# Attention block: maxima through GpSimd's DMA queue, scores seven pairs ahead, two buffers for the bias tables, slots written out

## The chip, the cores and the metric

The kernel runs on one core of one Trainium2 chip. Its time is device microseconds of one launch. Five engines work in parallel, each through its own instructions in order: TensorE (PE; PEld is its weight load), VectorE (DVE), ScalarE (ACT), GpSimd (POOL) and SyncE (SP), which here does nothing but issue DMAs. They meet at semaphores. Before the change three runs took 1225.28, 1225.32 and 1228.18 us; the median is 1225.32 us.

## The reference

Eight sequences of 512 tokens with 256 features go through a pre-norm layer: attention with 16 heads of 16 features and a bias by relative position, then a mixture of experts. All is float32. The part that matters here:

```
scores = einsum('bhqd,bhkd->bhqk', q, k) * SCALING + position_bias
attn   = softmax(scores, axis=-1)
ctx    = einsum('bhqk,bhkd->bhqd', attn, v)
x = x + ctx @ Wo.T
x = x + ffn(layernorm(x))      # 7 routed experts, two chosen, and a shared one
```

`position_bias` depends on key position minus query position alone, and is constant beyond a distance of about 90.

## The kernel before, in words

There are three stages, each a block that begins when all engines have ended the one before: `project` (norm, q, k, v and the bias tables; they go to DRAM), `attend` (attention) and `finish` (output projection and experts). The change lies in `attend` and in the loads that it shares with `project`.

`attend` handles 32 items, one for each of 8 sequences and 4 groups of 4 heads; item n is done in slot n. Eight items share a head group, so the bias tables of the group change when slots 8, 16 and 24 begin; four items are a quad. A slot has 8 steps; a step is one pair of heads and one block of 128 rows.

The softmax needs the row maxima before the exponentials, and for that the scores are computed twice. `scores` (L766) puts q times k of one head and 128 queries into one of three PSUM banks of `pS`; VectorE (L688) adds the bias from the table `near` and takes the negated maximum of each row into `nmax`. After the 16 units of an item `turn` (L692) splits the maxima into a high and a low part and transposes them, and two DMAs carry them by way of DRAM: `store_max` (L590) and, once that has landed, `load_max` (L597), which puts them as two more rows into `q_st`. `exponents` (L783, L791) computes the scores a second time, transposed, with the maxima and the far bias as additional rows and the near bias added through the table `bandT`; ScalarE takes the exponential (L733) into `prob`, and `values` (L805) multiplies with v one slot later, into `pC`. ScalarE copies `pC` out (`copy_ctx`, L742) and SyncE stores it. GpSimd copies v into its padded form (L670).

TensorE's order is written by hand: in step s of slot n it does the scores that lie LEAD = 5 steps beyond the next item's start, so those of item n+1, step s+5, or from step 3 on those of item n+2; then the exponents of slot n, step s; after each odd step a quarter of the values of item n-1. `PLACES` gives each of the 16 units of an item its bank; where it holds None a bank is left out, so that the pattern repeats after 18 places.

SyncE's queue carries everything: at the end of a slot the q, k, v rows of the item four slots on (`load_step`, L186 to L199: 8 DMAs of q and k rows of 4 KB each, two of far bias at times, one of v), then the store of the maxima, the store of the context, the loads of the maxima. The tables `near` and `bandT` have one buffer each; in the slot before the group changes the four loads of `near` wait until VectorE has done with the old one (L602 to L608), and those of `bandT` until TensorE has (L615 to L619). The first slots and the last four are written out; the 24 to 28 between them run in hardware loops, where semaphore values stand in registers.

Of the kernel before, what the change touches and what calls it, by code (L numbers as in the profile page):

```python
# [18 lines left out]
P = 128  # L19
# [66 lines left out]
def layer_kernel(nc, x, wqT, wkT, wvT, woT, rel_emb, gateT, expert_bias, w1, b1, w2, b2, low_rows,  # L86
# [19 lines left out]
    with top:  # L106
# [50 lines left out]
def attention_loads(g):  # L157
# [5 lines left out]
    def load_near(sp, quad, j):  # L163

        head = (quad // 2) * HPG + j
        rows = bass.AP(g["bias_dram"].tensor, head * VLEN, [[1, P], [1, TW]])
        sp.dma_start(near[:, j], rows).then_inc(near_ld[j], 16)

    def load_band(sp, quad, j):

        pair, side = divmod(j, 2)
        lead = ((quad // 2) * HPG + j) * VLEN + band_start(0)
        rows = bass.AP(g["bias_parts_dram"].tensor, lead, [[1, HALF], [H * VLEN, 2], [1, BW]])
        sp.dma_start(raw(bandT[HALF * side:HALF * side + HALF, pair]), rows).then_inc(band_ld[j], 16)
# [350 lines left out]
def attend(nc, mk, g):  # L525
# [8 lines left out]
    with ExitStack() as ctx:  # L534
# [19 lines left out]
        LEAD = 5  # L554

        PLACES = [0, 1, None, *range(2, 10), None, *range(10, 16)]
# [15 lines left out]
        with nc.Block() as block:  # L572
            @block.sync
            def _(sp):
# [12 lines left out]
                def store_max(m, par):  # L587

                    wait_apart(sp, passed, max_turned, m + 1)
                    sp.dma_start(max_dram[m].rearrange("a j (t i x) -> i (a j t) x", t=TT, i=4), turned[:, par]  # L590
                                 ).then_inc(max_out, 16)

                def load_max(m, r):
                    wait_apart(sp, passed, max_out, 16 * m + 16)
                    for side in range(2):
                        row = HALF * side + KQ
                        sp.dma_start(raw(q_st[row:row + KM, r]),  # L597
                                     max_dram[m].rearrange("a (p h) s -> h a p s", h=2)[side]).then_inc(max_ld, 16)

                def slot(s, u, quad, first=False, last=False, load=True, tables=False):  # L600
                    if u == 2 and tables:
                        wait_apart(sp, passed, max_done, MAX0 + 16 * (s + 1) + 8)  # L602
                        for j in range(2):
                            loads["near"](sp, quad + 1, j)
                    if not (last and u == 3):
                        store_max(s + 1, (u + 1) % 2)
                    if u == 2 and tables:
                        for j in range(2, HPG):  # L608
                            loads["near"](sp, quad + 1, j)
                    if not (first and u < 2):  # L610
                        wait_apart(sp, passed, evac, s - 1)
                        store_ctx(quad - (1 if u < 2 else 0), (u + 2) % 4, u % 2)
                    if not (last and u == 3):
                        load_max(s + 1, (u + 1) % 4)
                    if u == 3 and tables:  # L615
                        for pair in range(2):
                            wait_apart(sp, passed, e_mm, STEPS * s + TT * pair + TT)
                            for side in range(2):
                                loads["band"](sp, quad + 1, 2 * pair + side)  # L619
                    if load:  # L620
                        wait_apart(sp, passed, e_mm, STEPS * s + STEPS)
                        wait_apart(sp, passed, v_ready, s + 1)
                        loads["step"](sp, quad + 1, u, tables)

                store_max(0, 0)
                load_max(0, 0)
                for u in range(4):
                    slot(u, u, 0, first=True)
                with sp.Fori(0, HG - 1) as i:
                    for k in (1, 2):  # L630
                        for u in range(4):
                            slot(8 * i + 4 * k + u, u, 2 * i + k, tables=k == 1)
# [11 lines left out]
                for u in range(4):  # L644
                    slot(NI - 4 + u, u, QUADS - 1, last=True, load=False)
# [13 lines left out]
            @block.gpsimd  # L659
            def _(pool):  # L660
                for par in range(2):
                    pool.memset(v_aug[:, par].rearrange("p a b c -> p (a b c)"), 1.0).then_inc(ones_set, 1)
                wait_apart(pool, passed, ones_set, 2)

                with pool.Fori(0, QUADS) as i:
                    for u in range(4):
                        m = 4 * i + u
                        wait_apart(pool, passed, v_ld[u], 16 * (i + 1))
                        wait_apart(pool, passed, pv_done, PV0 + 4 * m - 4)
                        pool.tensor_copy(v_aug[:, u % 2, :, :, 0:DH],  # L670
                                         v_raw[:, u].rearrange("p (t h e) -> p t h e", t=TT, h=HPG)).then_inc(v_ready, 1)

            @block.vector
            def _(dve):
                dve.sem_inc(max_done, MAX0)

                def maxima(m, quad, new, step):

                    pair, t = divmod(step, TT)
                    for side in range(2):  # L680
                        j, r = 2 * pair + side, 2 * step + side
                        if new and t == 0:
                            dve.wait_ge(near_ld[j], 16 * (quad // 2 + 1))
                        unit = 16 * m + r
                        dve.wait_ge(s_mm, unit + 1)
                        wait_apart(dve, passed, max_done, MAX0 + unit - 3)
                        lead = P * t
                        dve.tensor_tensor_reduce(sums[:, r % 4], pS[:, BANK[r]], near[:, j, lead:lead + S], -1.0, BIG,  # L688
# [3 lines left out]
                def turn(m, par):  # L692

                    wait_apart(dve, passed, max_done, MAX0 + 16 * m + 16)
                    dve.tensor_copy(nparts[:, 0], nmax[:]).then_inc(split_done, 1)
                    wait_apart(dve, passed, split_done, 2 * m + 1)
                    dve.tensor_tensor(nparts[:, 1], nmax[:], nparts[:, 0], ALU.subtract).then_inc(split_done, 1)
                    wait_apart(dve, passed, split_done, 2 * m + 2)
                    if not (isinstance(m, int) and m < 2):
                        dve.wait_ge(max_out, 16 * m - 16)  # L700
                    dve.transpose(turned[:, par], raw(nparts[:].rearrange("p a j t -> p (a j t)"))).then_inc(max_turned, 1)

                def slot(n, u, quad, last=False):
                    for step in range(STEPS):
                        ahead, other = divmod(STEPS + step + LEAD, STEPS)
                        if not (last and u + ahead > 3):
                            maxima(n + ahead, quad + (u + ahead) // 4, u + ahead == 4, other)
                            if other == STEPS - 1:
                                turn(n + ahead, (u + ahead) % 2)

                for step in range(STEPS + LEAD):
                    maxima(step // STEPS, 0, step < STEPS, step % STEPS)
                    if step == STEPS - 1:
                        turn(0, 0)
                for u in range(4):
                    slot(u, u, 0)
# [600 lines left out]
```

## Time and profile before

| | |
|---|---|
| median of three runs | 1225.32 us |
| the profiled execution: its own time | 1226.09 us |
| its span | 1224.2 us |
| `project`, to the first maximum on VectorE | 117.2 us |
| `attend`, first exponents to last slot's end | 168.6 to 756.5 us |
| PE busy share of the span | 83% |
| mean granted TensorE clock | 0.914 |

The span is the stretch from the first to the last instruction; the execution's time has 1.9 us more around it. Slots are counted here by the start of their first exponents (L783), so slot 12 is 385.2 to 402.2. In a timeline row, the bracket at the end is the time that the engine sat idle before it and what ended that.

### The profile page before, as it was taken

Reading aid. Unit: us, or ns where it says so; the run is one execution under the profiler, and the core shown is the slowest. Engines: PE = TensorE matmul, PEld = TensorE weight load, DVE = VectorE, ACT = ScalarE, POOL = GpSimd, SP = SyncE. Lnnn points to the kernel's source line nnn. Section 1 sums busy time; section 2 is a strip of 40 time slices with the busy share of each in tenths; the row PEclk is TensorE's granted clock in tenths of the full one; section 3 lists DMA queues with packets and bytes.
Section 4 is the critical chain, followed back from the end, with each engine's and each line's share of the span. In section 5 each row is a group of like instructions: output and inputs, shape, how many; then the busy total and the mean of one; then the engine's idle time right before and its main releaser. Section 6 shows DMA issues by size and latency. Waiting matters only on the chain. (4 is left out here: it accounts for less than half of the span.)

```text
span 1224.2 us, 22575 instructions
## 1 busy us (share of the span) xinstructions
PE 1013.0 (83%) x7264; PEld 747.7 (61%) x7264; DVE 710.8 (58%) x2048; ACT 508.3 (42%) x680; POOL 52.3 (4%) x149
## 2 busy tenths in 40 slices
PE   5796348886798767888678868699999998999998
PEld 3685135544455434555345544488888888888887
DVE  5564436654466545665456642686666665676664
ACT  2342034543354424544344446454434343444433
POOL 1120000000000000000000000000000000000000
PEclk9898568988899978998789989699999999999999
DMA  5997312233222232222422232321110201011000
GB/s 119 316 318 245 91 32 67 80 92 96 70 73 78 77 104 68 78 71 70 109 79 78 75 100 75 112 69 36 35 56 14 70 12 59 17 52 35 2 18 18
DMA packets 65446, 99.94 MB, mean 82 GB/s; under 512 B 11000, under 2 KB 39184, under 8 KB 65342
## 3 DMA queue, kind: packets, MB, share of 16 engines
q1 hardware_dynamic: 65202, 98.53, 26.1%
q10 hardware_dynamic: 172, 0.56, 0.2%
q8 instruction: 32, 0.52, 0.2%
q14 instruction: 40, 0.33, 0.1%
HBM read 63.67 MB, written 34.93 MB: 81 GB/s over the span
## 5 line engine op out<-in xcount | busy, mean ns | idle before, releaser
L688 DVE CUSTOM_DVE_ANT_0 sums<-pS,near 128x512 bf16<-128x512 f32 x512 | 329.6, 688 | 272.1 <-PE pS L766 228.5
L733 ACT ACTIVATE prob<-pE 128x1024 f32<-128x1024 f32 x256 | 259.4, 1025 | 376.6 <-PE pE L791 376.3
L766 PE MATMUL pS<-k_st,q_st 48*128 48x512 f32 x512 | 183.3, 506 | 71.3 <-DVE nmax L688 47.0
L783 PE MATMUL pE<-q_st,k_st 62*128 62x512 f32 x512 | 144.6, 458 | 82.2 <-DMA q_st<-negated_maxima 51.2
L766 PEld LDWEIGHTS pS<-k_st,q_st 48*128 48x128 f32 x512 | 78.5, 203 | 216.8 <-DVE nmax L688 168.1
L1217 PE MATMUL pD<-w2p,h_p 128*128 128x256 f32 x1536 | 204.5, 287 | 4.9 <-DVE x L1067 4.9
L791 PEld LDWEIGHTS pE<-bandT,place 64*128 64x128 f32 x2048 | 198.3, 206 | 12.2
L1217 PEld LDWEIGHTS pD<-w2p,h_p 128*128 128x128 f32 x1536 | 192.9, 190 | 14.3 <-DVE x L1067 5.8
L1199 PE MATMUL pU<-x2T,w1p 128*128 128x512 f32 x768 | 191.5, 399 | 0.0
L791 PE MATMUL pE<-bandT,place 64*128 64x244 f32 (+2 forms) x2048 | 190.2, 288 | 0.0
L1130 ACT ACTIVATE h_f<-pU,b1s 128x512 f32<-128x512 f32 x128 | 88.1, 688 | 192.8 <-PE pU L1199 186.6
L1199 PEld LDWEIGHTS pU<-x2T,w1p 128*128 128x128 f32 x768 | 141.6, 190 | 29.3
L805 PE MATMUL pC<-prob,v_aug 128*32 128x512 f32 x1024 | 144.4, 639 | 11.3 <-ACT ctx_sb L742 11.3
L1067 DVE SCALAR_TENSOR_TENSOR x<-pD,combine,x 128x256 f32<-128x256 f32 x256 | 111.1, 479 | 64.6 <-PE pD L1217 63.0
L1056 DVE TENSOR_TENSOR h_p<-h_f,h_p 128x512 fp32r<-128x512 f32 x128 | 86.8, 690 | 71.0 <-ACT h_p L1133 66.0
L783 PEld LDWEIGHTS pE<-q_st,k_st 62*128 62x128 f32 x512 | 61.2, 203 | 95.4 <-issue 90.7
L1133 ACT ACTIVATE h_p<-pU,b1s 128x512 fp32r<-128x512 f32 x128 | 87.2, 681 | 0.0
L471 PE MATMUL pQ<-xT,w_p 128*128 128x512 f32 x192 | 52.4, 427 | 8.5 <-DVE qk L389 6.5
L471 PEld LDWEIGHTS pQ<-xT,w_p 128*128 128x128 f32 x192 | 38.1, 206 | 20.3 <-DVE qk L389 10.6
L688 DVE DVE_READ_ACCUMULATOR2_ANT nmax<- 128x1 f32 x512 | 42.6, 83 | 0.0
L805 PEld LDWEIGHTS pC<-prob,v_aug 128*32 128x32 f32 x1024 | 22.2, 112 | 29.0 <-ACT prob L733 13.7
L670 POOL COPY v_aug<-v_raw 128x256 f32<-128x256 f32 x32 | 12.8, 401 | 616.6 <-PE pC L805 594.1
(100 smaller groups left out, 525.8 us busy)
## 6 DMA issues: line engine op xcount, KB each, us to landing
x<-in_x SPq DMA_DIRECT2D x16, 512.0 KB, 4.7
q_parts<-qk SPq DMA_DIRECT2D x16, 512.0 KB, 5.2
k_parts<-qk SPq DMA_DIRECT2D x16, 512.0 KB, 4.8
q_st<-q_parts SPq DMA_DIRECT2D x64, 128.0 KB
k_st<-k_parts SPq DMA_DIRECT2D x64, 128.0 KB
ctx<-ctx_sb SPq DMA_DIRECT2D x32, 256.0 KB, 6.3
near<-bias_by_distance SPq DMA_DIRECT2D x16, 448.0 KB, 12.0
v_rows<-vs SPq DMA_DIRECT2D x8, 512.0 KB, 3.2
```

The costliest lines, as they stand in the source:

```text
L471: ins = pe.matmul(pQ[:, m % 2], w_p[:, a, w, c, P * h:P * h + P], xT[:, par, z, c], start=k == 0, stop=k == 5)
L688: dve.tensor_tensor_reduce(sums[:, r % 4], pS[:, BANK[r]], near[:, j, lead:lead + S], -1.0, BIG, ALU.add, ALU.min, nmax[:, j, t:t + 1]).th ...
L733: act.activation(prob[:, u % 2, 2 * step:2 * step + 2], pE[:, 2 * (step % 2):2 * (step % 2) + 2], ACT.Exp).then_inc(exp_done, 1)
L766: pe.matmul(pS[:, BANK[unit]], q_st[rows, r, pair, P * t:P * t + P], k_st[rows, r, pair], start=True, stop=True).then_inc(s_mm, 1)
L783: pe.matmul(pE[:, bank + side], k_st[rows, r, pair, P * t:P * t + P], q_st[rows, r, pair], start=True, stop=False, skip_group_check=True)
L791: ins = pe.matmul(pE[:, bank + side, a:z], place[rows, half], bandT[rows, pair, part, lead:lead + z - a], start=False, stop=half == 1 and ...
L805: ins = pe.matmul(pC[32 * j:32 * j + 32], v_aug[:, par, t, j], prob[:, par, at], start=t == 0, stop=t == TT - 1, skip_group_check=True)
L1067: dve.scalar_tensor_tensor(out=row, in0=pD[:, t // 2, t % 2], scalar=combine[:, par, t, e:e + 1], in1=row, op0=ALU.mult, op1=ALU.add).then ...
L1130: act.activation(h_f[:, e % 2, m], pU[:, e % 2, m], ACT.Gelu, bias=b1s[:, e, m:m + 1])
L1133: act.activation(h_p[:, e % 2, 0, m], pU[:, e % 2, m], ACT.Gelu, bias=b1s[:, e, m:m + 1]).then_inc(s["h_hi"], 1)
L1199: ins = pe.matmul(pU[:, e % 2, m], w1p[:, e, a, c, P * m:P * m + P], x2T[:, par, c, z], start=k == 0, stop=k == 5)
L1217: ins = pe.matmul(pD[:, t2, u], h_p[:, e % 2, a, m, P * t:P * t + P], w2p[:, e, z, m], start=k == 0 and e < NE - 1, stop=k == 5)
```

## The change

The maxima's DMAs move from SyncE to GpSimd's own queue, where they stand between the copies of v. LEAD goes from 5 to 7, with the left-out banks moved to match. `near` and `bandT` get a second buffer, chosen by the parity of the head group, and are loaded one of each per slot through the first quad of the group before. All loops of `attend` are written out, so every semaphore value is a constant. On ScalarE the copy of the context goes ahead of the first exponential of a slot.

```
-            near = sb("near", [P, HPG, TW], F32)
-            bandT = sb("bandT", [P, HPG // 2, 2, BW], F32R)
+            near = sb("near", [P, 2, HPG, TW], F32)
+            bandT = sb("bandT", [P, 2, HPG // 2, 2, BW], F32R)
...
-        LEAD = 5
-        PLACES = [0, 1, None, *range(2, 10), None, *range(10, 16)]
+        LEAD = 7
+        PLACES = [*range(6), None, *range(6, 14), None, 14, 15]
...
# SyncE
+                def slot(s, u, quad):
+                    hg = quad // 2
+                    if s >= 2:
+                        sp.wait_ge(evac, s - 1)
+                        store_ctx((s - 2) // 4, (u + 2) % 4, u % 2)
+                    if quad % 2 == 0 and hg < HG - 1:
+                        if hg >= 1:
+                            sp.wait_ge(max_done, MAX0 + 16 * 8 * hg)
+                            sp.wait_ge(e_mm, STEPS * 8 * hg)
+                        loads["near"](sp, hg + 1, u)
+                        loads["band"](sp, hg + 1, u)
+                    if quad < QUADS - 1:
+                        sp.wait_ge(e_mm, STEPS * s + STEPS)
+                        sp.wait_ge(v_ready, s + 1)
+                        loads["step"](sp, quad + 1, u, quad % 2 == 1)
...
# GpSimd
+                store_max(0)
+                load_max(0)
+                for m in range(NI):
+                    pool.wait_ge(v_ld[m % RING], 16 * (m // RING + 1))
+                    if m >= 2:
+                        pool.wait_ge(pv_done, PV0 + 4 * m - 4)
+                    pool.tensor_copy(v_aug[:, m % 2, :, :, 0:DH],
+                                     v_raw[:, m % RING].rearrange("p (t h e) -> p t h e", t=TT, h=HPG)).then_inc(v_ready, 1)
+                    if m < NI - 1:
+                        store_max(m + 1)
+                        load_max(m + 1)
...
# ScalarE
+                def slot(n):
+                    par = n % 2
                     for step in range(STEPS):
-                        if step == 0 and not (first and u < 2):
-                            act.wait_ge(pv_done, PV0 + 4 * n - 4)
+                        if step == 0 and n >= 2:
+                            copy_ctx(n - 2)
                         act.wait_ge(e_mm, STEPS * n + step + 1)
```

The places where instructions move are these. TensorE, the turn from one slot to the next, before (in the loop; MATMUL pC is the last quarter of the values, pS the scores, pE the exponents):

```order
L805 MATMUL pC<-prob,v_aug 32x512 x4
L765 REGISTER_ALU
L766 MATMUL pS<-k_st,q_st 128x512 [waits max_done]
L765 REGISTER_ALU
L766 MATMUL pS<-k_st,q_st 128x512 [waits max_done]
L777 REGISTER_ALU [waits far_loaded3]
L779 ISA [waits max_loaded]
L783 MATMUL pE<-q_st,k_st 128x512 [waits exp_done]
```

The same place now, on to the scores of the next step:

```order
L777 MATMUL pC<-prob,v_aug 32x512 x4
L738 MATMUL pS<-k_st,q_st 128x512 [waits max_done] x2
L755 MATMUL pE<-q_st,k_st 128x512 [waits exp_done,max_loaded,far_loaded3]
L755 MATMUL pE<-q_st,k_st 128x512
L763 MATMUL pE<-bandT,place 128x154 x4
L763 MATMUL pE<-bandT,place 128x218 x4
L738 MATMUL pS<-k_st,q_st 128x512 [waits max_done,qk_loaded1]
```

The scores ahead of the wait for the maxima are now the last two units of the next item, and the first scores of the item after it, with the wait for its q and k rows, come one step into the slot and no longer three. The register instructions are gone.

GpSimd in `attend`, before (one turn of its loop has four copies like these):

```order
L662 MEMSET v_aug 128x512 x2
L665 UNCONDITIONAL_BRANCH [waits ones_set]
L665 ISA
L670 COPY v_aug<-v_raw 128x16x16 [waits pv_done]
L670 COPY v_aug<-v_raw 128x16x16 [waits pv_done]
```

GpSimd now:

```order
L634 MEMSET v_aug 128x512 x2
L640 DMA negated_maxima<-turned 4x32x32 [waits max_turned,ones_set]
L647 DMA q_st<-negated_maxima 2x2x512 [waits max_out]
L647 DMA q_st<-negated_maxima 2x2x512
L656 COPY v_aug<-v_raw 128x16x16 [waits v_loaded0]
L640 DMA negated_maxima<-turned 4x32x32 [waits max_turned]
L647 DMA q_st<-negated_maxima 2x2x512 [waits max_out]
L647 DMA q_st<-negated_maxima 2x2x512
```

The store and the two loads of an item now stand in front of the copy of its v.

ScalarE at the start of a slot, before:

```order
L733 ACTIVATE prob<-pE 128x1024 [waits e_mm]
L731 ISA
L732 ISA [waits pv_done]
L733 ACTIVATE prob<-pE 128x1024 [waits e_mm]
L739 ISA
L742 ACTIVATE ctx_sb<-pC 128x512 [waits ctx_out1,pv_done]
```

ScalarE now:

```order
L709 ACTIVATE prob<-pE 128x1024 [waits e_mm] x8
L717 ACTIVATE ctx_sb<-pC 128x512 [waits ctx_out1,pv_done]
L709 ACTIVATE prob<-pE 128x1024 [waits e_mm] x8
L717 ACTIVATE ctx_sb<-pC 128x512 [waits ctx_out0,pv_done]
```

The copy (L742, now L717) has gone from behind the first exponential of a slot to ahead of it.

## Rows read from the trace of the kernel before

**Rows 1.** Waits of the whole span: who for whom, total us, times, longest.

```profile
PE pE L783 <- DMA q_st<-negated_maxima: 51.2, 19, 21.4
DVE sums L688 <- DMA near<-bias_by_distance: 34.8, 8, 11.5
PE pE L783 <- DMA bandT<-bias_parts_by_distance: 18.0, 3, 6.1
PE pC L805 <- ACT ctx_sb L742: 11.3, 17, 1.0
```

**Rows 2.** Windows by slot: length; busy PE, PEld, DVE, ACT, POOL; PEclk, DMA share, GB/s.

```profile
385.20:402.20 17.00, 13.94 (x128) 8.47 (x128) 10.96 (x35) 8.48 (x9) 0.40 (x1) 1.00 0.23 73
420.10:449.70 29.60, 16.67 (x128) 10.37 (x130) 9.73 (x31) 8.57 (x9) 0.04 (x1) 0.77 0.41 107
449.70:471.00 21.30, 14.36 (x130) 8.62 (x127) 12.19 (x39) 8.55 (x9) 0.76 (x2) 0.89 0.28 80
694.70:719.00 24.30, 15.03 (x130) 9.57 (x130) 10.78 (x35) 8.59 (x9) 0.40 (x1) 0.79 0.53 150
719.00:734.20 15.20, 14.95 (x128) 9.77 (x130) 9.62 (x31) 8.59 (x9) 0.04 (x1) 0.89 0.10 30
```

**Rows 3.** Timeline of slot 12 to 13: SP's issues, VectorE's transpose, TensorE's first exponents.

```profile
384.07 0.65 SPq L186 DMA_DIRECT2D q_st<-q_parts  x1
391.72 0.21 DVE L701 STREAM_TRANSPOSE turned<-nparts 128x32 f32<-128x32 f32 x1 [0.22 <-DVE nparts L697]
392.98 0.67 SPq L590 DMA_DIRECT2D negated_maxima<-turned  x1
398.94 1.57 SPq L597 DMA_DIRECT2D q_st<-negated_maxima  x2
401.02 0.65 SPq L186 DMA_DIRECT2D q_st<-q_parts  x1
402.24 0.50 PE L783 MATMUL pE<-q_st,k_st 62*128 62x512 f32 x2 [1.77 <-DMA q_st<-negated_maxima]
```

**Rows 4.** DMA view of 384 to 400 us: GB/s in 40 slices of 0.4 us.

```profile
GB/s 0 20 0 20 31 164 164 10 61 41 61 72 195 184 21 41 105 287 79 61 41 61 41 82 41 66 77 205 410 92 61 41 61 38 41 44 46 5 0 0
```

**Rows 5.** DMA view of 156 to 162 us: queue, packets, MB, share of 16 engines.

```profile
q1 hardware_dynamic: 90, 0.31, 12.7%
```

**Rows 6.** TensorE's timeline: three rows in the loop, then three in a written-out slot.

```profile
389.17 0.40 PE L783 MATMUL pE<-q_st,k_st 62*128 62x512 f32 x2
390.39 0.65 PE L783 MATMUL pE<-q_st,k_st 62*128 62x512 f32 x2
393.60 0.54 PE L783 MATMUL pE<-q_st,k_st 62*128 62x512 f32 x2
...
203.70 0.40 PE L783 MATMUL pE<-q_st,k_st 62*128 62x512 f32 x2
204.66 0.73 PE L783 MATMUL pE<-q_st,k_st 62*128 62x512 f32 x2
207.18 0.49 PE L783 MATMUL pE<-q_st,k_st 62*128 62x512 f32 x1
```

**Rows 7.** Timeline of the start of `attend`: first scores of item 1, transpose, maxima's DMAs, exponents.

```profile
130.01 0.21 DVE L701 STREAM_TRANSPOSE turned<-nparts 128x32 f32<-128x32 f32 x1
138.99 0.79 PE L766 MATMUL pS<-k_st,q_st 48*128 48x512 f32 x2 [10.41 <-DMA k_st<-k_parts]
145.82 1.40 PE L766 MATMUL pS<-k_st,q_st 48*128 48x512 f32 x2 [0.43 <-DVE nmax L688]
153.12 0.65 SPq L590 DMA_DIRECT2D negated_maxima<-turned  x1
168.65 0.80 PE L783 MATMUL pE<-q_st,k_st 62*128 62x512 f32 x2 [21.42 <-DMA q_st<-negated_maxima]
```

**Rows 8.** One line's durations over the span, min, median, max ns: L670, then L695.

```profile
L670 POOL COPY v_aug<-v_raw x32: 397/401/402, 117.4 to 745.9; 128x256 f32<-128x256 f32 x32
L695 DVE CAST nparts<-nmax x32: 174/175/177, 129.6 to 739.6; 128x16 fp32r<-128x16 f32 x32
```

More of the change, by code:

```diff
@@ L585, in store_ctx @@
                     sp.dma_start(ctx_dram[4 * (quad % 2) + r, quad // 2], ctx_sb[:, par]).then_inc(c_out[par], 16)
[L587 to L623, printed above, removed]
@@ L634, in _ @@
+                for quad in range(QUADS - 1):
+                    for u in range(4):
+                        slot(4 * quad + u, u, quad)
                 sp.dma_start(g["wo_f"][:], g["woT"].rearrange("(c p) o -> p c o", p=P)).then_inc(g["small_ld"], 16)
@@ L644, in _ @@
                 for u in range(4):
-                    slot(NI - 4 + u, u, QUADS - 1, last=True, load=False)
+                    slot(NI - 4 + u, u, QUADS - 1)
                     if u == 1:
@@ L700, in turn @@
+                    if m >= 2:
                         dve.wait_ge(max_out, 16 * m - 16)
[L701 to L709, printed above, removed]
@@ L711, in _ @@
-                for step in range(STEPS + LEAD):
-                    maxima(step // STEPS, 0, step < STEPS, step % STEPS)
-                    if step == STEPS - 1:
-                        turn(0, 0)
-                for u in range(4):
-                    slot(u, u, 0)
-                with dve.Fori(1, QUADS - 1) as i:
-                    for u in range(4):
-                        slot(4 * i + u, u, i)
-                for u in range(4):
-                    slot(NI - 4 + u, u, QUADS - 1, last=True)
-                    if u == 2:
-                        dve.wait_ge(den_ld, 16)
-                        dve.reciprocal(den[:], den[:]).then_inc(den_inv, 1)
+                    dve.transpose(turned[:, m % 2], raw(nparts[:].rearrange("p a j t -> p (a j t)"))).then_inc(max_turned, 1)
@@ L726, in _ @@
+                for ahead in range(STEPS * NI):
+                    m, step = divmod(ahead, STEPS)
+                    maxima(m, step)
+                    if step == STEPS - 1:
+                        turn(m)
+                dve.wait_ge(den_ld, 16)
+                dve.reciprocal(den[:], den[:]).then_inc(den_inv, 1)
             @block.scalar
             def _(act):
-                def slot(n, u, quad, first=False):
+                def slot(n):
+                    par = n % 2
                     for step in range(STEPS):
-                        if step == 0 and not (first and u < 2):
-                            act.wait_ge(pv_done, PV0 + 4 * n - 4)
+                        if step == 0 and n >= 2:
+                            copy_ctx(n - 2)
@@ L746, in _ @@
-                with act.Fori(1, QUADS) as i:
-                    for u in range(4):
-                        slot(4 * i + u, u, i)
-                copy_ctx(NI - 2, 0, NI // 2 - 1)
-                copy_ctx(NI - 1, 1, NI // 2 - 1)
+                for n in range(NI):
+                    slot(n)
+                copy_ctx(NI - 2)
+                copy_ctx(NI - 1)
             @block.tensor
```

83 lines of the change are left out of this document (35 added, 48 removed).

## The prediction

> **What bounds the kernel now.** I first read the waits of the whole span [rows 1]. TensorE stands 51.2 us before the exponents for the DMA that brings the maxima, 18.0 us for the band table and 11.3 us for the context copy; VectorE stands 34.8 us for `near`, and TensorE behind it. All of this is in `attend`, between 168.6 and 756.5 us. Then I cut that stretch at the first exponents of each slot. Slots 1 to 29 run from 180.9 to 734.2, so 553.3 us, 19.1 each. A plain slot (slot 12) takes 17.0 us with TensorE busy for 13.9; slot 14, where `near` is changed, takes 29.6, slot 15, where the band is, 21.3, and slot 28, ahead of whose maxima SyncE issues the weights, 24.3 [rows 2]. No engine is full: VectorE has 11.0 and ScalarE 8.5 us of work in 17.0.
>
> What sets the 17.0 is found in the timeline of slot 12 [rows 3]. The maxima of item 13 are transposed at 391.7, which is 6.5 us into the slot; their store is issued at 393.0 and landed only when the load is issued, at 398.9; 3.3 us later the exponents start. So 6.5 + 10.5 = 17.0, round and round. Of the 10.5, 5.9 are the store of 16 KB. The DMA view says why: the queue works off the q and k rows issued from 384.07 on, most of the time at 40 to 60 GB/s, and is down to 5 GB/s only at 398.8 [rows 4]. The last of that are the maxima and then the context's part for the engines that are behind (two of 16, so 32 of 256 KB, at 45 GB/s 0.7 us; the maxima's 0.4), so the step load itself ends near 397.6. In a quiet stretch the same kind of load shows 12.7% of 16 engines, which is two engines [rows 5]. The store stands in the same queue behind what these two still have to move, and lands 1.3 us after they end. The step load thus takes 13.5 us from its issue, 12.1 of them with these two engines at work.
>
> A sentence of the Trainium skill agrees with the 12.7%: by DMA: Bandwidth & Descriptors (Why a DMA increments its semaphore by 16 and not by 1), the slowest dimension of the pattern sets how many engines share a copy, and that is 2 for the rows copied twice.
>
> **The change part by part.**
>
> Written-out slots and the context copy set the work of a slot, W. From 389.17 to 390.39 and on to 393.60 two steps take 1.22 and 3.21 in the loop; in a slot that is written out already they take 0.96 and 2.52 [rows 6]. The first comes twice a slot, so register waits cost about 2 x 0.26 + 0.69 = 1.2 us. The context copy moves ahead of the exponential and removes 0.7 a time (11.3 / 17). From 17.0 take the 1.8 that stand before the exponents [rows 3], 1.2 and 0.7: 13.3. TensorE's busy time of 13.9 in slot 12 is the other end, and has stretches in it where a matmul is only late. I take W = 13.8, since rows nearest to it are the busy time.
>
> LEAD = 7. The last scores of the next item come in step 0, ahead of the wait for the maxima, and no longer in step 2. Step 2 began 4.0 us after step 0 (389.17 against 385.2), so the transpose comes 2.5 us into the slot. Until the next slot wants the maxima there are 13.8 - 2.5 = 11.3 us. The scores now want q and k of the item after next one step into a slot; that load is issued about 1.1 us before the slot ahead of it starts (384.07 against 385.2) and needs 13.5 + 1.3 to land. Allowed are 1.1 + 13.8 + 0.75 = 15.65, so it fits with 0.9 us to spare when nothing stands before it.
>
> The maxima on GpSimd's queue. No row shows a DMA issued by GpSimd. Call R the time from transpose to exponents, 10.5 now. Lower end: the store lands 1.3 us after the queue is free, its issue takes 1.2, the loads 3.3, so 5.8. Upper end: it still waits for the two busy engines, now from 2.5 us into the slot until these end at 12.4 (13.5 - 1.1), 1.3 to land and 3.3 for the loads: landed 17.0 into the slot, R = 14.5; that is without any cost of GpSimd's own. I take 11.8: halfway that would be 10.2, and I add 1.6 for the issue of three DMAs by GpSimd, a guess the size of SP's own issue of the two loads, 1.57 [rows 3]. A stall here doesn't repeat in full, as the next item's transpose is already out when TensorE waits: a slot takes (W + 2.5 + R) / 2 where R is over 11.3. That is 14.05, or 0.25 x 18 = 4.5 us in the 18 slots without tables. GpSimd's copies of v, 0.40 each [rows 8], stand behind the loads of the maxima and have a slot of slack.
>
> By DMA: Bandwidth & Descriptors (Queues, rings and completion order) each DMA engine takes turns between its queues by packets, which speaks for the lower half of this range; no row here shows two queues at work.
>
> Two buffers for the tables. The long slots vanish: over 17.0 they are 12.6 and 4.3 us at one change of group [rows 2], there are three changes, and slot 28 gives 7.3; together about 58. But the tables share a queue with the step load. The two busy engines have 12.1 us of that load in each slot. A context of 256 KB, `near` 448 and band 122 are 0.83 MB, at the peak of 410 GB/s [rows 4] 2.0 us, and the maxima and far rows some 0.9: 15.0 us of work for a slot of 13.8. The spare 0.9 is soon used up, so in slots 1 to 3, 8 to 11 and 16 to 19 the loads bound: 11 x 15.0 = 165.0. Without tables it is 12.1 + 0.6 + 0.4 = 13.1, under W. The other 18 take 18 x 13.8 = 248.4.
>
> The start. The maxima of item 0 are ready at 130.0, but SyncE gets to their store at 153.1, behind three step loads, and the exponents begin at 168.65 after 21.4 us of idle time [rows 7]. GpSimd can issue it at once; even with R at 20 it is there at 150. Then the scores decide: 12 units from 138.99 to 146.5, now 16, so 4 x 0.63 more and the start is at about 150.5. The third load ends near 150, which is just in time. Saved: 18.1. Slot 0 stays at 12.3.
>
> The end. Slots 30 and 31 have no loads; each loses only the 0.7 of the copy: 1.4. `finish` is untouched. Code written out must be fetched; the 15.2 us of slot 29 with its 128 matmuls, all of it written out, has TensorE busy for 14.95 [rows 2], so I cost it at nothing.
>
> **The sum.** 553.3 - 165.0 - 248.4 = 139.9; with the start 18.1 and the end 1.4 it is 159.4; less 4.5 for the maxima, 154.9. The profiled execution took 1226.1, which leaves 1071.2; the median of the runs is 0.8 lower. Forecast 1070.5 us.
>
> **Rivals.**
>
> A. The queue takes the maxima's place fully: with the maxima's small packets between them and no idle gaps, the two engines need more for a step load, say 14.4 us, which is the 13.5 and the 0.9 by which slot 13 is longer than slot 12 (402.24 to 420.1 [rows 2, 3]). Then every loaded slot takes 15.5 instead of 13.8 or 15.0: 16 x 1.7 + 11 x 0.5 = 33, so 1104. For it speaks that the spare is thin; against it that the gaps between SP's issues are part of the 12.1.
>
> B. The round trip stays the bound. With R = 18 a slot takes (13.8 + 2.5 + 18) / 2 = 17.15, what it is now; what is left are tables, slot 28, start and end, 58 + 18 + 1.4 = 77: 1225.3 - 77 = 1148. It needs a store on GpSimd's queue to cost 7.5 us more than now, though it no longer stands at the end of a queue.
>
> C. GpSimd's issue is starved and the kernel gets slower. To lose the 77 us again, slots would have to take 2.6 us more than 17.15, so R at 23. With R = 30 a slot takes 23.15 and the sum is 1148 + 29 x 6 = 1322. The mechanism would be VectorE holding off GpSimd. Against it: GpSimd's copies take 397 to 402 ns in all 32 slots beside VectorE's 512 maxima, and the only casts of VectorE here take 175 ns, once a slot [rows 8]. SBUF — State Buffer of the Trainium skill (Who interferes with whom, and the trap named under the doors) says that VectorE's two-port modes lock GpSimd out of the port by which it writes descriptors, and gives about 3.1 us for a DMA of 0.62 us. By that price R would rise by some 7.5 us for three DMAs, to rival B; the even copy times agree with its other rule, that an instruction with one SBUF input doesn't contend.
>
> D. All better: W = 13.3 and loads that overlap well, 27 x 13.3 + 2 x 13.3 = 386 for the 29 slots: 1226 - 167 - 19.5 = 1039.
>
> **How the numbers follow.** Forecast 60%, A 18%, B 8%, C 3%, D 10%, and 1% that no more than half a rival's gain is left. The forecast's own range is 1055 to 1090. The range reaches from 1042 to 1125: it leaves out D's far end, B and C. 0.3% of the time is about what can be told from no change; faster by more than that has 0.96, within it 0.01, slower 0.03, since only C lies on that side and B is 6% away.
>
> **What would show it.** In the profile of the changed kernel: first exponents at 150 and no idle time of 20 us before them; plain slots of 13.8 to 14.1 with the granted clock near 1.0 and TensorE busy nearly throughout; slots 1 to 3, 8 to 11 and 16 to 19 near 15, with TensorE's wait named after `k_st` or `q_st` at the scores; waits for `near` and band gone; store issue to load issue on GpSimd at 4 to 7 us, and R below 12. If plain slots take 15 and over with waits at the scores, A holds; if they take 17 with the maxima named, B. The forecast is wrong if slots without tables stay above 14.8, or if TensorE's own work with no wait is outside 13.3 to 13.9.

## The result and the profile after

The changed kernel takes 1060.38 us (median of four runs, 1056.83 to 1065.39), against 1226.51 us for the kernel before in the same comparison: a ratio of 0.865, 95% interval 0.860 to 0.869. The forecast was 1070.5 with a range of 1042 to 1125. The profiled execution has a span of 1055.7 us, which is 168.5 less than the profiled one before. The sums below are of these two executions; by the medians it is 166.1 less.

The waits of the whole span show first what is gone. These are all that is left in the attention block of the kinds in [rows 1], with what took their place:

```profile
PE pS L738 <- DMA k_st<-k_parts: 27.4, 13, 10.9
PE pC L777 <- ACT ctx_sb L717: 1.0, 1, 1.0
PE pE L755 <- DMA q_st<-negated_maxima: 0.4, 2, 0.2
PE pE L755 <- issue: 2.8, 4, 1.3
DVE sums L678 <- DMA near<-bias_by_distance: 1.2, 2, 0.8
```

The 51.2 us for the maxima are 0.4 by name. With them belong the 2.8 us of the fourth line, for which the profile names nothing ("issue"); why is shown at slot 8 below. The 11.3 us for the context copy are 1.0, `near` has 1.2 us left, all of it before the first exponents, and the band table is named no more. Of the 13 waits for k rows at the scores, the one at the start (10.9 us) was there before (10.4); twelve are new, 16.5 us in sum.

The windows of slots 2, 9, 10, 14 and 28 (columns as in [rows 2]):

```profile
176.40:192.80 16.40, 14.98 (x132) 8.93 (x130) 10.78 (x35) 8.83 (x10) 2.21 (x5) 0.90 0.39 113
276.00:289.20 13.20, 13.20 (x128) 8.27 (x128) 10.51 (x35) 8.33 (x10) 1.89 (x4) 1.00 0.44 131
289.20:306.10 16.90, 14.99 (x130) 9.20 (x130) 10.78 (x35) 8.77 (x10) 2.16 (x5) 0.90 0.37 114
348.50:362.10 13.60, 13.60 (x132) 8.55 (x132) 10.72 (x35) 8.89 (x10) 2.27 (x5) 1.00 0.32 99
544.30:559.40 15.10, 13.77 (x132) 8.57 (x130) 12.00 (x39) 9.21 (x10) 2.50 (x5) 1.00 0.57 149
```

Slots 9 and 14 are TensorE from end to end: 13.2 of 13.2, 13.6 of 13.6. Slots 2 and 10 hold a wait for k rows; slot 28, which took 24.3 [rows 2], takes 15.1, with a wait for the maxima at its end.

The timeline of slot 8 (262.36 to 275.95), by VectorE's transpose, GpSimd's issues and the first exponents of slot 9, answers to [rows 3]:

```profile
263.95 0.21 DVE L691 STREAM_TRANSPOSE turned<-nparts 128x32 f32<-128x32 f32 x1
264.46 0.69 POOL L640 DMA_DIRECT2D negated_maxima<-turned  x1 [2.17 <-DVE turned L691]
270.73 1.08 POOL L647 DMA_DIRECT2D q_st<-negated_maxima  x2 [5.58 <-DMA negated_maxima<-turned]
275.95 0.50 PE L755 MATMUL pE<-q_st,k_st 62*128 62x512 f32 x2 [0.17 <-issue]
```

Transposed 1.6 us into the slot, stored 0.5 later, loads issued after another 6.3. The time from issue to landing as min, median and max, first for the store over the whole span (L640), then for the two loads of this slot (L647):

```profile
DMA to landing us min/median/max: 4.0/5.6/6.4
DMA to landing us min/median/max: 2.2/3.4/4.6
```

The exponents wait for both loads. The second is issued at 271.27 (270.73 and half of 1.08) and lands 4.6 us later, at 275.86; the exponents start 0.09 us behind it. So the round trip from transpose to landing is 11.9 us, and it ends with the slot, not before it. (The median over all 64 loads is 2.5 us, but both of a pair are there only some 5 us after the first is issued.) For the maxima of items 4 to 28 it is 11.5 us at the median (11.0 to 12.6). In eight slots TensorE stood idle until 0.09 or 0.25 us after this landing, mostly for 0.1 to 0.3 us, and longest at the ends of slots 25 and 28, where the profile names nothing either:

```profile
517.58 0.50 PE L755 MATMUL pE<-q_st,k_st 62*128 62x512 f32 x2 [1.00 <-issue]
559.37 0.50 PE L755 MATMUL pE<-q_st,k_st 62*128 62x512 f32 x2 [1.33 <-issue]
```

The start answers to [rows 7]:

```profile
126.55 0.21 DVE L691 STREAM_TRANSPOSE turned<-nparts 128x32 f32<-128x32 f32 x1
127.38 0.91 POOL L640 DMA_DIRECT2D negated_maxima<-turned  x1 [13.55 <-DVE turned L691]
132.94 1.10 POOL L647 DMA_DIRECT2D q_st<-negated_maxima  x2 [4.65 <-DMA negated_maxima<-turned]
136.27 1.22 PE L738 MATMUL pS<-k_st,q_st 48*128 48x512 f32 x3 [10.90 <-DMA k_st<-k_parts]
146.37 1.00 PE L755 MATMUL pE<-q_st,k_st 62*128 62x512 f32 x2
```

The maxima are there 7.3 us before the exponents begin, at 146.4 instead of 168.65, with no idle time ahead of them.

The 168.5 us by stretch: the first exponents come 22.3 us earlier and slot 0 is 2.6 longer (14.9 for 12.3); slots 1 to 29 take 411.4 us instead of 553.3, so 141.9 less; slot 30 is 10.1 instead of 11.4; from the start of slot 31 (745.6 and 582.7) to the end are 473.0 us instead of 478.6. 22.3 - 2.6 + 141.9 + 1.3 + 5.6 = 168.5.

### The profile page after: what moved, and what is told of

Read it like the earlier page. It is cut to its first block and busy times, and to the rows that moved or that the text cites. A ratio compares the mean times of both kernels' runs of the same rounds, so it can differ in the third digit from the quotient of the medians.

```text
span 1055.7 us, 20280 instructions
## 1 busy us (share of the span) xinstructions
PE 969.4 (92%) x7264; PEld 721.2 (68%) x7264; DVE 704.8 (67%) x2048; ACT 514.2 (49%) x680; POOL 109.4 (10%) x245
## 5 line engine op out<-in xcount | busy, mean ns | idle before, releaser
L678 DVE CUSTOM_DVE_ANT_0 sums<-pS,near 128x512 bf16<-128x512 f32 x512 | 325.3, 687 | 125.4 <-PE pS L738 123.7
L738 PE MATMUL pS<-k_st,q_st 48*128 48x512 f32 x512 | 167.2, 497 | 40.6 <-DMA k_st<-k_parts 27.4
L763 PEld LDWEIGHTS pE<-bandT,place 64*128 64x128 f32 x2048 | 182.5, 190 | 16.1
L738 PEld LDWEIGHTS pS<-k_st,q_st 48*128 48x128 f32 x512 | 72.3, 193 | 171.5 <-DVE nmax L678 128.1
L763 PE MATMUL pE<-bandT,place 64*128 64x244 f32 (+2 forms) x2048 | 180.1, 272 | 0.0
L755 PE MATMUL pE<-q_st,k_st 62*128 62x512 f32 x512 | 138.8, 425 | 3.5 <-issue 2.8
L777 PE MATMUL pC<-prob,v_aug 128*32 128x512 f32 x1024 | 137.2, 610 | 1.0 <-ACT ctx_sb L717 1.0
L1024 DVE TENSOR_TENSOR h_p<-h_f,h_p 128x512 fp32r<-128x512 f32 x128 | 86.8, 690 | 67.7 <-ACT h_p L1101 65.3
L647 POOL DMA_DIRECT2D q_st<-negated_maxima x64 | 34.8, 548 | 165.2 <-DMA negated_maxima<-turned 165.2
L470 PEld LDWEIGHTS pQ<-xT,w_p 128*128 128x128 f32 x192 | 37.4, 202 | 19.9 <-DVE qk L388 10.2
L212 POOL TENSOR_SCALAR rtmp<-mv 128x4 f32<-128x4 f32 x16 | 5.8, 364 | 422.8 <-DVE mv L944 358.9
## 6 DMA issues: line engine op xcount, KB each, us to landing
near<-bias_by_distance SPq DMA_DIRECT2D x16, 448.0 KB, 14.2
```

Of the source, the lines that this page charges most:

```text
L470: ins = pe.matmul(pQ[:, m % 2], w_p[:, a, w, c, P * h:P * h + P], xT[:, par, z, c], start=k == 0, stop=k == 5)
L738: pe.matmul(pS[:, BANK[unit]], q_st[rows, r, pair, P * t:P * t + P], k_st[rows, r, pair], start=True, stop=True).then_inc(s_mm, 1)
L755: pe.matmul(pE[:, bank + side], k_st[rows, r, pair, P * t:P * t + P], q_st[rows, r, pair], start=True, stop=False, skip_group_check=True)
L763: ins = pe.matmul(pE[:, bank + side, a:z], place[rows, half], bandT[rows, (quad // 2) % 2, pair, part, lead:lead + z - a], start=False, st ...
L777: ins = pe.matmul(pC[32 * j:32 * j + 32], v_aug[:, par, t, j], prob[:, par, at], start=t == 0, stop=t == TT - 1, skip_group_check=True)
```

## The experiments

Times are medians of four runs, ratios against the kernel before measured on the same chip. The changed kernel's ratio is 0.865, and 0.01 of it is 12 us. R stands for the time from transpose to exponents, as in the prediction, or to the landing of both loads where the exponents come later.

**One part undone at a time.** First the queue. SyncE's slot gets its old commands back, GpSimd keeps the copies. The wait for `e_mm` before the loads is new; it is over long before they are issued:

```
                     hg = quad // 2
+                    if s + 1 < NI:
+                        store_max(s + 1)          # on SyncE
                     if s >= 2:
                         sp.wait_ge(evac, s - 1)
                         store_ctx((s - 2) // 4, (u + 2) % 4, u % 2)
+                    if s + 1 < NI:
+                        sp.wait_ge(e_mm, STEPS * s + 1)
+                        load_max(s + 1)
```

> The changed kernel with one part undone: the maxima's store and loads are issued by SyncE again, in the old place between the step loads. Theory (the store stands behind the step load in one queue, and SyncE gets to it only after nine issues): a slot is again 13.5 from the issue of the step load, 1.3 to land, 3.3 for the loads, less 1.1, so near 17.0 in spite of LEAD = 7; 27 slots x about 3, start and slot 28 lost again: 1150 to 1180 us. Rival (seven pairs of lead are slack enough for the round trip, whatever the queue): waits for the maxima stay away, 1060 to 1080 us.

Measured: 1182.7 us, 0.966 (0.963 to 0.970). The changed kernel without the new queue is only 41 us faster than the kernel before, so the lead of seven pairs can't have bought much there. The timeline of item 14's maxima, transposed at the end of slot 12 (SyncE's store and loads, TensorE's first exponents of slot 14):

```profile
394.80 0.21 DVE L706 STREAM_TRANSPOSE turned<-nparts 128x32 f32<-128x32 f32 x1
400.67 0.57 SPq L589 DMA_DIRECT2D negated_maxima<-turned  x1
410.50 1.26 SPq L596 DMA_DIRECT2D q_st<-negated_maxima  x2
413.56 0.79 PE L770 MATMUL pE<-q_st,k_st 62*128 62x512 f32 x2 [2.40 <-issue]
```

The transpose is early and then waits 5.9 us until SyncE has issued the step load, and the store takes 9.8 us behind it. Slots without tables are near 17.0, as expected. Eleven slots with tables in the queue (2 to 4, 9 to 12, 17 to 20) take about 19 us, which the expectation had left out; that is 22 us, more than the 3 by which the time is over its range.

Second the lead:

```
-        LEAD = 7
-        PLACES = [*range(6), None, *range(6, 14), None, 14, 15]
+        LEAD = 5
+        PLACES = [0, 1, None, *range(2, 10), None, *range(10, 16)]
```

> The changed kernel with LEAD = 5 and the old bank places. Theory (the transpose then comes 6.3 us into the slot, and the round trip on GpSimd's queue is about 9.2): 15.5 us a slot instead of 14.2 on the mean, and TensorE waits for the maxima in every slot: 1090 to 1105 us. Rival (with its own queue the round trip is short enough without the lead, or the step loads bound anyway): 1060 to 1067 us.

Measured: 1105.4 us, 0.906 (0.900 to 0.911), at the upper edge of the range. The mean of slots 1 to 29 is 15.8 us (expected 15.5), but they are less even than expected. Slot 13:

```profile
357.50 0.50 PE L755 MATMUL pE<-q_st,k_st 62*128 62x512 f32 x2 [0.76 <-issue]
362.59 0.21 DVE L691 STREAM_TRANSPOSE turned<-nparts 128x32 f32<-128x32 f32 x1
363.10 0.69 POOL L640 DMA_DIRECT2D negated_maxima<-turned  x1 [6.23 <-DVE turned L691]
368.56 1.09 POOL L647 DMA_DIRECT2D q_st<-negated_maxima  x2 [4.77 <-DMA negated_maxima<-turned]
371.95 0.51 PE L755 MATMUL pE<-q_st,k_st 62*128 62x512 f32 x2 [0.98 <-issue]
```

5.1 to the transpose and 9.4 for the round trip make 14.4, a loss of 1 us; but with tables on the way (slots 8 and 10) the round trip is longer, and these slots take 17.6 and 17.7. Slot 25 takes 19.1: its store is issued 2.4 us after the transpose, and the round trip is 13.9. The expectation took R to be 9.2 in the changed kernel too, which is what the median landing of the loads (2.5 us) gives; it is 9.1 here at the median, but 11.5 there. The lead brings the transpose some 3 us forward in the slot and the landing by 1: it is 14.4 us into slot 13 here and 13.5 into slot 8 there.

Third the tables, with `near[:, 0]`, `bandT[:, 0]` and the loads back in the last two slots of a group:

```
-                    if quad % 2 == 0 and hg < HG - 1:
...
+                    if quad % 2 == 1 and hg < HG - 1 and u == 2:
+                        for j in range(HPG):
+                            sp.wait_ge(max_done, MAX0 + 16 * (s + 1) + (8 if j < 2 else 16))
+                            loads["near"](sp, hg + 1, j)
```

> The changed kernel with one buffer for near and band, loaded at the change of the group as before. Theory (the waits of VectorE and TensorE at the three changes come back, some 12 and 4 us each, less what the step loads no longer lose to tables): 1095 to 1115 us, with the slots 0 to 4 and 8 to 13 shorter than in the changed kernel. Rival (the lead of seven pairs covers part of the table's load): under 1080 us.

Measured: 1110.0 us, 0.907 (0.903 to 0.910). As expected: slots 6, 14 and 22 take 31.5 to 32.0 us, and the ones behind them 15.8 to 17.0. The loads show their other side: slots 1 to 4 take 13.6, 13.5, 13.5, 13.5 us where the changed kernel's took 15.2, 16.4, 13.5, 14.7. Of slots 8 to 13, 10, 12 and 13 are shorter too; 8 and 9 are not.

```profile
DVE sums L680 <- DMA near<-bias_by_distance: 52.4, 8, 16.7
PE pS L740 <- DMA k_st<-k_parts: 13.6, 2, 11.2
```

Fourth ScalarE's order:

```
                         if step == 0 and n >= 2:
-                            copy_ctx(n - 2)
+                            act.wait_ge(pv_done, PV0 + 4 * n - 4)
                         act.wait_ge(e_mm, STEPS * n + step + 1)
...
                                        ACT.Exp).then_inc(exp_done, 1)
+                        if step == 0 and n >= 2:
+                            copy_ctx(n - 2)
```

> The changed kernel with ScalarE's copy of the context behind the first exponential of a slot again. Theory (TensorE waits 0.7 us for it in each slot, and is the bound in most): 30 x 0.7 = 20, so 1075 to 1083 us. Rival (the wait falls into slots where the loads bind, or is hidden by the scores): 1060 to 1066 us.

Measured: 1069.0 us, 0.873 (0.870 to 0.876): between the two. The wait is back, 23 times and 13.0 us, and plain slots take 14.1 instead of 13.5. Slots 1 to 29 are 10.3 us longer in sum, not 17 (0.6 each), partly because the longer slots give the loads time: the waits for k rows behind the start are 14.1 us instead of 16.5, those for the maxima 1.1 instead of 3.2. The interval of its ratio only just clears that of the changed kernel: 9 us by the medians, some 3 to 17 if both intervals are counted.

**One part done alone on the kernel before.** All loops written out as plain ones, nothing else:

```
-                with pe.Fori(1, QUADS - 1) as i:
+                for i in range(1, QUADS - 1):
```

> The kernel before with its loops of the attention block written out and nothing else changed. Theory (a slot of 17.0 us is a round of step load, store and loads of the maxima, in which TensorE's register waits don't stand): no change or a few us less, 1215 to 1228 us. Rival (the 1.2 us of register waits come off every slot): 24 x 1.2 = 29 less, 1197 us.

Measured: 1198.7 us, 0.980 (0.977 to 0.983). My theory fell and the rival's number came, by another sum, so that was luck. The profiled execution is 30.3 us shorter: 4.3 at the start, 19.6 in slots 1 to 29 and 6.4 behind the start of slot 31. The 4.3 are not the edit's, since the first scores of `attend` already come 4.1 us earlier. Slots 12 and 13 take 16.6 us instead of 17.0 and 17.9, with a wait at the end as before. Two rows of SyncE and TensorE at the end of slot 13:

```profile
405.62 1.26 SPq L597 DMA_DIRECT2D q_st<-negated_maxima  x2
408.39 0.50 PE L783 MATMUL pE<-q_st,k_st 62*128 62x512 f32 x2 [1.57 <-issue]
```

From the loads to the exponents are 2.8 us, not 3.3, and SyncE issues the two loads in 1.26 us, not 1.57 [rows 3]. On the mean of slots 3 to 27 the transpose comes 0.4 us earlier in the slot, the store follows it 0.3 sooner, the exponents follow the loads 0.3 sooner, and from store to loads it is 0.2 longer: 0.8 us in all, not 1.2. SyncE works with registers in the loop as well, and its issues are links of the round; I had looked for loop costs on TensorE alone.

Then the maxima on GpSimd's queue alone, in loops, with LEAD = 5 and single tables (SyncE also gets a wait for VectorE before two of the table loads, where its wait for the store had stood; the comment in the lines is mine):

```
+                store_max(0, 0)
+                load_max(0, 0)
+                with pool.Fori(0, QUADS - 1) as i:
+                    for u in range(4):
+                        slot(i, u)                # copy of v, store_max, load_max
```

> The kernel before with the maxima's DMAs on GpSimd's queue and nothing else changed (LEAD = 5, loops, one buffer for the tables). Theory: a plain slot is 6.5 to the transpose and 9.2 for the round trip, 15.7 instead of 17.0; first exponents at about 150 instead of 168.6; slot 28 loses its 7 us; tables as before: 1155 to 1175 us. Rival (the queue is not what holds the store, GpSimd's is as slow): within 25 us of before, all of it from the start.

Measured: 1180.9 us, 0.965 (0.963 to 0.968), 6 us over the range. The first exponents come at 145.3, before the 150 expected, but slot 0 takes 18.0 us instead of 12.2; slot 28 takes 18.3 (expected 17); the plain slots are at 15.9 to 16.5 where 15.7 was expected. It is 43 us, where undoing the same part in the changed kernel costs 122: alone it runs into the late transpose and the tables.

**The two engines.** In a step load four of the DMAs write 32 partitions from 16 rows, each row into two partitions. They are split by rows:

```
-            sp.dma_start(raw(q_st[row:row + 2 * DH, r]).rearrange("p j s -> p (j s)"),
-                         stacked(q_dram, b, hg, side, 0, 2)).then_inc(qk_ld[r], 16)
+            for lead in (row, row + DH):
+                sp.dma_start(raw(q_st[lead:lead + DH, r]).rearrange("p j s -> p (j s)"),
+                             stacked(q_dram, b, hg, side, 0, 1)).then_inc(qk_ld[r], 16)
```

and k the same, first in the kernel before.

> The kernel before, but each q or k load that writes its rows twice (32 partitions from 16 rows, in one DMA) is split into two DMAs of 16 rows. Theory (a copy of that form is worked by two engines, and the maxima's store waits behind these): the step load ends soon after its last issue, the store lands in 2 to 3 us, and a plain slot is bound by TensorE at 14.5 to 15 us; start earlier by some 15: 1125 to 1160 us. Rival (the load is bound by its bytes or by SyncE's issues, which are 13 instead of 9): 1215 us or more.

Measured: 1112.1 us, 0.908 (0.905 to 0.911), better than expected. The same bytes and four more DMAs per step take 111 us off; between the profiled executions it is 24.9 at the start and 86.8 in slots 1 to 29. From the store of the maxima to the issue of their load are 2.2 us instead of 5.9, on SyncE's queue and with LEAD = 5:

```profile
348.29 0.21 DVE L703 STREAM_TRANSPOSE turned<-nparts 128x32 f32<-128x32 f32 x1 [0.22 <-DVE nparts L699]
348.74 0.67 SPq L592 DMA_DIRECT2D negated_maxima<-turned  x1
350.97 1.51 SPq L599 DMA_DIRECT2D q_st<-negated_maxima  x2
```

The slots no longer wait for it, so they show what the loop costs a slot that TensorE sets: slot 3, written out, and slot 13, in the loop.

```profile
183.50:197.60 14.10, 13.64 (x130) 8.44 (x128) 10.69 (x35) 8.49 (x9) 0.42 (x2) 1.00 0.31 87
341.90:357.00 15.10, 14.25 (x132) 8.80 (x130) 10.81 (x35) 8.63 (x9) 0.43 (x2) 1.00 0.30 87
```

The same split in the changed kernel:

> The changed kernel with the same split of the q and k loads. Theory (13 waits for k rows, 27.4 us in sum, come from two engines that are full): they go, slots 1 to 27 all near 13.4 us, 1035 to 1048 us. Rival (bytes or SyncE's issues bound): 1060 us or more.

Measured: 1022.3 us, 0.835 (0.833 to 0.837), the fastest of all, 38 us under the changed kernel and 13 us faster than its range. The expectation had counted the slots alone: of the 34.7 us between the profiled executions 19.6 lie in slots 1 to 29, but 12.1 are the earlier start (134.2 instead of 146.4) and 3.3 slot 0. Every slot from 2 to 27 takes 13.5 us; two of them:

```profile
267.30:280.80 13.50, 13.50 (x130) 8.46 (x128) 10.69 (x35) 8.79 (x10) 2.16 (x5) 1.00 0.50 135
280.80:294.30 13.50, 13.50 (x131) 8.44 (x128) 10.69 (x35) 8.82 (x10) 2.19 (x5) 1.00 0.53 135
```

The DMA view, 40 slices of a table slot (8 in the changed kernel, 10 here), GB/s:

```profile
GB/s 229 133 133 12 60 133 72 24 217 84 171 74 48 121 142 250 398 373 127 171 314 337 316 200 90 91 60 133 185 186 72 60 48 60 60 48 48 48 48 42
```

```profile
GB/s 158 61 158 73 158 170 158 61 194 194 61 161 196 146 134 134 73 234 404 364 165 32 235 320 287 267 187 159 105 142 17 0 0 0 0 0 0 24 0 170
```

The first ends in a tail, mostly at 40 to 60 GB/s, that never comes to rest; in the second, seven of the last nine slices are at zero.

A control cuts the same DMAs in two along the columns, so that as many are issued and each still reads its rows twice:

```
+            for j in range(2):
+                sp.dma_start(raw(q_st[row:row + 2 * DH, r, j]),
+                             halved(q_dram, b, hg, side, j)).then_inc(qk_ld[r], 16)
```

> Control for the split by rows: the changed kernel with the same loads cut into as many DMAs, but along the columns, so that each still writes 32 partitions from 16 rows. Theory (such a copy runs on two engines whatever its size): the waits for k rows stay near 27 us and the time is that of the changed kernel, 1055 to 1072 us. Rival (more and smaller DMAs are what helped): under 1040 us.

Measured: 1069.2 us, 0.874 (0.871 to 0.877), with the waits for k rows at 26.2 us. More and smaller DMAs don't help; how a copy lies over the engines does.

**What is left of the change's parts once the loads are spread.** The edits are those shown above, on top of the split by rows.

> The changed kernel with the rows split and the maxima's DMAs back on SyncE. Theory (the queue hurt only because of the two engines' backlog): plain slots at 13.5 with no wait for maxima; what stays lost is the start, where SyncE is behind its step loads (9 us), and slot 28, behind the weights (3 to 7 us): 1033 to 1041 us. Rival (SyncE gets to the store too late behind 13 issues): slots over 14.5, 1055 us or more.

Measured: 1038.2 us, 0.849 (0.846 to 0.852), as the theory had it: plain slots are 13.5 and one wait for the maxima remains, in slot 28, behind the weights (7.0 us; the slot takes 18.8 instead of 13.6); the first exponents come at 141.9 instead of 134.2.

> The changed kernel with the rows split and LEAD = 5. Theory (the round trip of the maxima is 6.6 us once their store waits for nobody, and five pairs leave 7.2): no waits, 1022 to 1026 us. Rival (the lead is needed for itself): 29 slots over 14.2, 1040 us or more.

Measured: 1029.8 us, 0.841 (0.839 to 0.844), 4 us over the range. Plain slots are at 13.6 and R is 6.7 us at the median, but the waits for the maxima are not all gone. At slot 9, with table loads on the way, R is 10.4, and TensorE stands at the end of the slot:

```profile
270.29 0.50 PE L757 MATMUL pE<-q_st,k_st 62*128 62x512 f32 x2 [2.15 <-issue]
```

Slots 9 and 10 take 15.8 and 14.8 us, which is 3.6 of the 5.8 that slots 1 to 29 are longer; slot 28 is 1.0 longer, slot 0 1.3, slot 30 0.9, and the start comes 1.1 earlier.

> The changed kernel with the rows split, LEAD = 5 and the maxima on SyncE: of the change only the tables, the written-out slots and the order on ScalarE are left. Theory: plain slots 13.5, start and slot 28 lost, 1033 to 1045 us, so that neither of the two measures against the round trip is worth more than the start and slot 28. Rival: with 13.5 us slots the round trip doesn't fit any more and they take 14.5 or more, 1060 us.

Measured: 1042.5 us, 0.852 (0.850 to 0.855), as expected: with neither of the two measures against the round trip the plain slots take 13.6 us, 9 and 10 among them, and slot 28 waits 9.9.

## Why the prediction was right, and where not

*The bound.* That the round of the maxima sets 17.0 us, and that its store is held up by the two busy engines and by SyncE's order, is shown from both sides: put back on SyncE's queue the plain slots are 17 again with all else in place, and with the copies spread they need neither the new queue nor the lead.

*W.* I took 13.8 between 13.3 and 13.9; it is 13.5. TensorE's busy time in slot 12 held matmuls that were only late, so the estimate from the intervals of the written-out slots [rows 6] was the better one. Of its parts, the loop costs a slot 1.0 us (15.1 against 14.1), where I had 1.2, and the context copy 0.6, where I had 0.7. Writing out was not undone in the changed kernel; the 1.0 is from the kernel before with spread loads.

*Tables and loads.* That the step loads become a bound in the table slots was right in the sum and wrong in the place: the 11 slots took 159.9 us (predicted 165.0), the other 18 took 251.5 (predicted 248.4 and 4.5 for the maxima). The backlog has to build up first. Rival A's 15.5 us in every loaded slot did not come: plain slots are at 13.5. In slots 8 and 9 nobody waits for k rows; in the later quads the waits come at the ends of the table quads and in the quads after them (12, 13, 20, 21: 14.2 to 15.0).

*The maxima on GpSimd.* The size was right: R is 11.5 at the median, forecast 11.8 (halfway between my bounds was 10.2), and TensorE stands 3.2 us for the maxima (0.4 by name, 2.8 without), forecast 4.5. The working was not, so the closeness is partly luck. GpSimd's issues take 0.7 us for the store and 1.1 for both loads, against SyncE's 0.67 and 1.57 [rows 3], which my 1.2 and 3.3 already held; the 1.6 that I added on top stands for nothing. What fills its place are the two busy engines, also for DMAs from a queue of their own: the store takes 5.6 us to land, and 3.2 in the kernel with the spread loads, where R is 8.0. Rivals B and C have nothing for them: R is nowhere near 18, and no issue by GpSimd took over 0.91 us.

*The start.* Predicted 18.1 saved with slot 0 unchanged; measured 22.3 less 2.6. The first exponents don't wait for the third load and slot 0 does: its first step takes 4.7 us, 2.2 of them a wait for k rows. The prediction's own sum has a slip of 1.5: 16 units of 0.63 from 138.99 on end at 149.0, not at 150.5. The same 0.63 holds in the result, where 16 units take from 136.27 to 146.4. The other 2.7 are that `attend` began earlier (136.27 against 138.99 for the same matmul). They are not the change's: the first scores of `attend` come at 116.2 in the profiled execution of the kernel before, the latest of all, and at 111.7 to 114.7 in the thirteen others, with and without the change. Why they differ is open.

*The end.* 6.9 us instead of 1.4. Slot 30 gives 1.3 of it. Slot 31 to the end of the program is 5.6 us shorter, 4.5 of them after the last context copy, so in `finish`, which I had at nothing. In the profile of the kernel before, VectorE stands there once for 3.4 us, for nothing that the profile names, and TensorE behind it:

```profile
1016.60 1.29 DVE L1056 TENSOR_TENSOR h_p<-h_f,h_p 128x512 fp32r<-128x512 f32 x2 [3.37 <-issue]
1018.74 1.57 PE L1217 MATMUL pD<-w2p,h_p 128*128 128x256 f32 x8 [3.41 <-DVE x L1067]
```

The same gap of 3.3 to 3.4 us stands at the same instruction in the two other kernels whose `attend` has loops, and in none of the eleven that are written out. From the last context copy to the end the three take 460.2 to 462.0 us, the eleven 455.6 to 457.9. So it goes with the loops; the kernel with nothing but its loops written out shows it too (455.6). What in the looped program makes VectorE stand is open.

So 13.6 us more came off between the profiled executions than forecast, and 10 by the medians: 6.5 in slots 1 to 29, 1.6 at the start, 5.5 at the end. What each part is worth inside the changed kernel: queue 122, tables 50, lead 45, ScalarE's order about 9. That is more than the 166 gained together, because each of them alone lets the same round or queue bind again. The lead, the tables and the order were not tried alone on the kernel before.

## What to carry to other kernels

When a transfer of some KB takes 6 us, look at what stands ahead of it in its queue and over how many DMA engines that is spread, before moving it or giving it more lead: here four DMAs per step written with a repeated row kept two of 16 engines busy for 12 us, and splitting them by rows gained 111 us in the old kernel and 38 in the new. A part's worth read from one undone and one done alone can differ threefold (the queue: 122 and 43 us). In a round that passes through a DMA queue, the loop overhead of the engine that issues counts as well as that of the engine that computes. And where two loads share a semaphore, ask when both have landed: the median of 2.5 us hid that here, and a wait for which the profile names nothing was for the second of them.

## What the runs showed of the hardware

- A short wait can cost more than itself. In slot 10 of the changed kernel TensorE waited 1.9 us for k rows:

```profile
292.08 0.80 PE L738 MATMUL pS<-k_st,q_st 48*128 48x512 f32 x2 [1.91 <-DMA k_st<-k_parts]
```

  and the slot took 16.9 us, 3.4 more than 13.5: its granted clock is 0.90 in the windows above, and the matmul of that row takes 0.80 us where the rows at full clock have 0.50. The clock stood at its lower level (1.2 GHz) from 291.9 to 295.3. The same happened in slot 2, where a wait of 1.4 us made the slot 2.9 longer. But it doesn't follow each such wait: waits of 1.7, 1.4 and 1.6 us in slots 18, 19 and 20 cost about themselves (15.2, 14.8, 15.0), and the clock stayed at 1.00.
- A DMA on GpSimd's own queue is not free of the backlog of SyncE's: it lands in 5.6 us against 3.2 for the same store. Without the backlog SyncE's is the faster: in the kernel with spread loads the load of the maxima is issued 2.2 us after the store from SyncE and 3.5 us after it from GpSimd, at the median.
- In all eight runs with the maxima on GpSimd's queue the store in slot 25 is late, and no later or earlier one behind the first is: 2.4 us behind the transpose instead of 0.5 (2.9 instead of at most 1.0 in the looped kernel), with GpSimd idle for nothing that the profile names:

```profile
504.88 0.21 DVE L691 STREAM_TRANSPOSE turned<-nparts 128x32 f32<-128x32 f32 x1
507.27 0.70 POOL L640 DMA_DIRECT2D negated_maxima<-turned  x1 [4.06 <-issue]
```

  It is in loops and written out alike; the cause is open.
- Writing out 32 slots, with some 250 TensorE instructions in each, showed no stall of TensorE for code: slots at 13.50 us with TensorE busy for 13.50.
